# A 4-bit code table built from two-slope planes with min and max: four ScalarE and four VectorE operations per chunk in place of six and six, and no GpSimd subtraction

## The reference

```python
w = NF4[codes]                      # 16 values from -1.0 to 1.0
w = w.reshape(O, I // 64, 64) * scales[:, :, None]
q, k, v = (lin_lora(x, W, A, B) for each of three)      # 512 x 512 each
o  = lin_lora((q + k + v) / 3, W_o, ...);   x1 = x + o
g, u = lin_lora(x1, W_g), lin_lora(x1, W_u)             # 1792 x 512 each
d  = lin_lora(silu(g) * u, W_d, ...);       r = x1 + d  # W_d is 512 x 1792
x  = layernorm(x + r)
x  = layernorm(x + ffn(x))          # ffn: one more coded matrix, absmax scales
```

## Time and profile before

| | us |
|---|---|
| median of 3 runs | 570.43 (570.41 to 571.09) |
| span of the profiled execution | 569.6 |
| TensorE matmul busy | 506.0 (89%) |
| VectorE busy | 434.0 (76%) |
| ScalarE busy | 362.1 (64%) |
| GpSimd busy | 335.2 (59%) |

### The profile page before, as it was taken

The page is one execution under the profiler, slowest core; times in us unless marked ns, Lnnn a source line. Parts: engine busy times, 40 slices in busy tenths (PEclk is TensorE's granted clock), DMA queues, the critical chain, the costliest instruction groups (busy, mean ns, idle before and its releaser), DMA issues.

```text
span 569.6 us, 8051 instructions
## 1 busy us (share of the span) xinstructions
PE 506.0 (89%) x2260; PEld 398.3 (70%) x2260; DVE 434.0 (76%) x821; ACT 362.1 (64%) x655; POOL 335.2 (59%) x318
## 2 busy tenths in 40 slices
PE   0465549988999999999999999989999799999995
PEld 0142338766788878777777787768888588888874
DVE  7899988999857779989899899257745885465542
ACT  8899956698757668878789686216768542232121
POOL 5889824179857678979879789314739811020011
PEclk9986659999999999999999999999999999999999
DMA  8732402033323122323323230064000000010011
GB/s 249 256 100 86 129 18 67 13 99 119 100 69 93 56 93 96 107 82 112 106 91 108 80 112 20 1 249 148 2 0 2 0 2 1 18 39 20 0 37 38
DMA packets 20379, 42.97 MB, mean 75 GB/s; under 512 B 3312, under 2 KB 3440, under 8 KB 19824
## 3 DMA queue, kind: packets, MB, share of 16 engines
q1 hardware_dynamic: 20112, 42.09, 23.1%
q0 software_dynamic: 224, 0.38, 0.3%
HBM read 40.36 MB, written 2.10 MB: 75 GB/s over the span
## 4 chain that ended last, share of the span: by engine, by line
PE 68%; POOL 15%; issue 13%; ACT 2%; DVE 2%; POOLq 0%; ACTq 0%; DVEq 0%
PE bank L870 58%; POOL wf L615 6%; PE bank L1002 3%; POOL wf L623 3%; POOL wf L628 2%; PE bank L961 2%; POOL wf L634 2%; PE bank L987 1%; PE bank L1106 1%; PE bank L888 1%; PE bank L895 1%; ACT prob L831 1%; ACT pT_hi L681 0%; PE bank L889 0%; DVE rmax L1312 0%
## 5 line engine op out<-in xcount | busy, mean ns | idle before, releaser
L702 ACT ACTIVATE bank<-code 128x512 f32<-128x512 int32 x372 | 207.8, 595 | 25.1 <-DVE half L1165 12.1
L615 POOL TENSOR_TENSOR wf<-halves 128x512 f32<-128x512 f32 x62 | 80.1, 1292 | 78.5 <-DVE halves L1169 77.3
L870 PE MATMUL bank<-x_hi,gu_hi 128*128 128x512 f32 x224 | 89.5, 399 | 2.7 <-POOL gu_lo L641 2.7
L664 POOL TENSOR_TENSOR rstd<-veps,neg_half 128x1 f32<-128x1 f32 x32 | 17.6, 549 | 121.7 <-issue 110.5
L870 PE MATMUL bank<-x_lo,gu_hi 128*128 128x512 f32 x224 | 87.3, 390 | 0.0
L870 PE MATMUL bank<-x_hi,gu_lo 128*128 128x512 f32 x224 | 87.3, 390 | 0.0
L1165 DVE SCALAR_TENSOR_TENSOR half<-half,bank 128x512 f32<-128x512 f32 x124 | 81.5, 680 | 3.6 <-ACT bank L702 3.6
L1163 DVE SCALAR_TENSOR_TENSOR half<-code,bank 128x512 f32<-128x512 int32 x124 | 79.2, 680 | 6.5 <-ACT bank L702 5.1
L1169 DVE TENSOR_TENSOR halves<-half,bank 128x512 f32<-128x512 f32 x124 | 79.3, 680 | 0.0
L623 POOL TENSOR_TENSOR wf<-wf,scale 128x512 f32<-128x512 f32 x50 | 65.3, 1305 | 3.9
L870 PEld LDWEIGHTS bank<-x_hi,gu_hi 128*128 128x128 f32 x224 | 42.1, 188 | 16.6 <-issue 6.3
(11 more groups left out here) (195 smaller groups left out, 1133.7 us busy)
## 6 DMA issues: line engine op xcount, KB each, us to landing
code<-codes SPq DMA_DIRECT2D x62, 256.0 KB, 2.7
scale<-scales SPq DMA_DIRECT2D x100, 128.0 KB, 2.9
xs<-xT SPq DMA_DIRECT2D x1, 2048.0 KB, 12.9
ea_raw<-ex_A SPq DMA_DIRECT2D x1, 2048.0 KB, 9.6
eb_raw<-ex_B SPq DMA_DIRECT2D x1, 2048.0 KB, 7.7
out<-rows SPq DMA_DIRECT2D x8, 256.0 KB, 2.0
bgu_raw<-loB_gu SPq DMA_DIRECT2D x1, 1792.0 KB, 10.5
wqkv_raw<-w_qkv SPq DMA_DIRECT2D x1, 768.0 KB, 4.0
```

What stands on the lines that cost most here:

```text
L615: pool.tensor_tensor(w, halves[:, j % 2, 0, :], halves[:, j % 2, 1, :], ALU.subtract).then_inc(diff_done, 1)
L664: pool.tensor_tensor(rstd[:, s:s + 1], veps[:, s:s + 1], neg_half[:, :], ALU.pow)\
L702: nc.scalar.activation(plane[m % RING_PLANE][:, :], src, func, bias=float(start), scale=float(slope)).then_inc(plane_ready, 1)
L870: last = nc.tensor.matmul(ps, a, b, start=start and i == 0 and n == 0, stop=stop and i == len(terms) - 1 and n == 2)
```

## The change

The 16 table values are now built from three bent lines ("two-slope planes": ScalarE's Prelu with a slope on either side, `BEND_LOW`, `BEND_LAST`, `BEND_TOP`), one Relu and the code itself, joined by two min and two max. All values are scaled by `GAIN`, so that the code itself is one of the lines; the factor is taken out again in `m1`, `p`, `silu`, `h`, `down` and the layer norm of the ffn, and a unit matrix times `GAIN` (`gain_eye`) takes the place of `ident` there. The chunk's last VectorE operation is an item of its own, `out`, that stands one half later; merges and splits stand one half later too. GpSimd only multiplies.

```diff
 def half(c, part):
     if part == 1:
+        due.append([1, ("out", c)])
         if c in MERGED:
-            due.append([2, ("merge", c)])
+            due.append([3, ("merge", c)])
         if c in SPLIT:
-            due.append([3 if c in MERGED else 2, ("split", c)])
+            due.append([4 if c in MERGED else 3, ("split", c)])
...
-plane = bank[0:RING_PLANE]
+last_ps, mid_ps, top_ps = bank[0:3]
...
 # ScalarE
+act.wait_ge(eye_in, 16)
+nc.scalar.activation(gain_eye[:, :], ident[:, :], ACT.Copy, scale=GAIN).then_inc(gain_set, 1)
...
+if item[2] == 0:
+    act.wait_ge(codes_in[j % RING_CODES], 16 * (j // RING_CODES + 1))
+    if j >= 2:
+        act.wait_ge(low_done, j - 1)
+    bent_plane(bent[:, j % 2, :], src, BEND_LOW, bent_ready)
+    if j:
+        act.wait_ge(low_done, j)
+    bent_plane(last_ps[:, :], src, BEND_LAST, last_ready)
+    if j:
+        act.wait_ge(clip_done, j)
+    nc.scalar.activation(mid_ps[:, :], src, ACT.Relu, bias=..., scale=...).then_inc(mid_ready, 1)
+else:
+    if j:
+        act.wait_ge(value_done, j)
+    bent_plane(top_ps[:, :], src, BEND_TOP, top_ready)
...
 # VectorE
+    if item[2] == 0:
+        dve.wait_ge(bent_ready, j + 1)
+        dve.wait_ge(last_ready, j + 1)
+        nc.vector.scalar_tensor_tensor(lj, bent[:, j % 2, :], ..., last_ps[:, :], ALU.add, ALU.min).then_inc(low_done, 1)
+        dve.wait_ge(mid_ready, j + 1)
+        nc.vector.scalar_tensor_tensor(mid_ps[:, :], code[...], float(CODE_SHIFT), mid_ps[:, :], ALU.add, ALU.max).then_inc(mid_done, 1)
+    else:
+        nc.vector.scalar_tensor_tensor(lj, lj, float(BEND_LAST[3]), mid_ps[:, :], ALU.add, ALU.min).then_inc(clip_done, 1)
+elif kind == "out":
+    dve.wait_ge(top_ready, j + 1)
+    dve.wait_ge(clip_done, j + 1)
+    nc.vector.scalar_tensor_tensor(value[:, j % 2, :], top_ps[:, :], float(BEND_TOP[3]), low[:, j % 2, :], ALU.add, ALU.max).then_inc(value_done, 1)
...
 # GpSimd
-pool.tensor_tensor(w, halves[:, j % 2, 0, :], halves[:, j % 2, 1, :], ALU.subtract).then_inc(diff_done, 1)
-pool.tensor_tensor(w, w, scale[:, i % RING_CODES, :], ALU.mult).then_inc(done, 1)
+pool.tensor_tensor(w, v, scale[:, i % RING_CODES, :], ALU.mult).then_inc(scaled_done, 1)
...
 # VectorE: merge (v, o, d) and h; down is changed in the same way
-nc.vector.tensor_tensor(w, lora_ps[:, :], w, ALU.add)
+nc.vector.scalar_tensor_tensor(w, lora_ps[:, :], GAIN, w, ALU.mult, ALU.add)
-nc.vector.tensor_tensor(a, a, unit_ps[(2 * n + 1) % 3][:, :], ALU.mult)
+nc.vector.scalar_tensor_tensor(a, unit_ps[(2 * n + 1) % 3][:, :], 1.0 / GAIN, a, ALU.mult, ALU.mult)
```

More of the change, by code:

```diff
@@ L58, with line, crossing, bend @@
        0.7229568362236023, 1.0]
-def line(sign, a, b):
-    slope = sign * (NF4[b] - NF4[a]) / (b - a)
-    return slope, sign * NF4[a] - slope * a
-UPPER = [line(1, 8, 9), line(1, 10, 11), line(1, 12, 13), line(1, 14, 15)]
-LOWER = [line(-1, 6, 5), line(-1, 4, 3), line(-1, 2, 1), (1.5 * (NF4[0] - NF4[1]), -NF4[0])]
+def line(a, b):
+    slope = (NF4[b] - NF4[a]) / (b - a)
+    return slope, NF4[a] - slope * a
+def crossing(left, right):
+    at = (right[1] - left[1]) / (left[0] - right[0])
+    return at, left[0] * at + left[1]
+def bend(left, right):
+    at, value = crossing(left, right)
+    return GAIN * right[0], -GAIN * right[0] * at, left[0] / right[0], GAIN * value
+FREE = 0.5
+GAIN = 1.0 / line(10, 11)[0]
+FIRST = ((line(1, 2)[0] * FREE + line(1, 2)[1] + 1.0) / FREE, -1.0)
+BEND_LOW = bend(line(3, 4), line(5, 6))
+BEND_LAST = bend(FIRST, line(1, 2))
+BEND_TOP = bend(line(12, 13), line(14, 15))
+RELU_MID = (GAIN * line(8, 9)[0], GAIN * line(8, 9)[1])
+CODE_SHIFT = GAIN * line(10, 11)[1]
+def lut_table(prelu_as_relu=False):
+    table = []
+    for c in range(16):
+        def plane(b):
+            x = b[0] * c + b[1]
+            return max(x, 0.0) + (0.0 if prelu_as_relu else min(x, 0.0) * b[2])
+        low = min(plane(BEND_LOW) + BEND_LOW[3] - BEND_LAST[3], plane(BEND_LAST))
+        mid = max(c + CODE_SHIFT, max(RELU_MID[0] * c + RELU_MID[1], 0.0))
+        clip = min(low + BEND_LAST[3], mid)
+        table.append(max(plane(BEND_TOP) + BEND_TOP[3], clip) / GAIN)
+    return table
 GROUPS = [range(f, f + 2) for f in range(0, NF, 2)]
@@ L98 @@
 RING_W = 3
-RING_PLANE = 3
 RING_H = 5
@@ L272, in build @@
         scale = at("scale", 6, [P, RING_CODES, 512])
-        half = at("half", 12, [P, 2, 512])
-        halves = at("halves", 16, [P, 2, 2, 512])
+        low = at("low", 12, [P, 2, 512])
+        bent = at("bent", 16, [P, 2, 512])
+        value = at("value", 20, [P, 2, 512])
         wf = at("wf", 24, [P, RING_W, 512])
@@ L601, in _ @@
             pool.memset(neg_half[:, :], -0.5).then_inc(neg_half_set, 1)
-            mults = 0
+            sums = 0
             for item in filter(None, V):
                 kind = item[0]
-                if kind == "lut" and item[2] == 1:
+                if kind == "out":
                     c = item[1]
                     j = CHUNKS.index(c)
-                    w = wf[:, j % RING_W, :]
-                    pool.wait_ge(lut_step, 6 * (j + 1))
+                    w, v = wf[:, j % RING_W, :], value[:, j % 2, :]
+                    pool.wait_ge(value_done, j + 1)
                     if j >= RING_W:
@@ L1152, in _ @@
                     j = CHUNKS.index(c)
-                    src = code[:, j % RING_CODES, :]
-                    dve.wait_ge(codes_in[j % RING_CODES], 16 * (j // RING_CODES + 1))
-                    for i in range(3 * item[2], 3 * item[2] + 3):
-                        m, side = 6 * j + i, i % 2
-                        lines = (UPPER, LOWER)[side]
-                        ps, acc = plane[m % RING_PLANE][:, :], half[:, side, :]
-                        dve.wait_ge(plane_ready, m + 1)
-                        if m >= 2:
-                            dve.wait_ge(lut_step, m - 1)
-                        if i < 2:
-                            ins = nc.vector.scalar_tensor_tensor(acc, src, float(lines[3][0]), ps, ALU.mult, ALU.max)
-                        elif i < 4:
-                            ins = nc.vector.scalar_tensor_tensor(acc, acc, float(lines[3][1]), ps, ALU.add, ALU.max)
-                        else:
-                            if j >= 2:
-                                dve.wait_ge(diff_done, j - 1)
-                            ins = nc.vector.tensor_tensor(halves[:, j % 2, side, :], acc, ps, ALU.max)
-                        ins.then_inc(lut_step, 1)
+                    lj = low[:, j % 2, :]
@@ L1191, in _ @@
                     dve.wait_ge(xhi_done, item[1] + 1)
-                    low(x_lo[:, k, tk], xs[:, k, tk], x_hi[:, k, tk], xlo_done)
+                    rest(x_lo[:, k, tk], xs[:, k, tk], x_hi[:, k, tk], xlo_done)
                 elif kind == "m1":
@@ L1225, in _ @@
                     dve.wait_ge(p_ready, NB)
-                    low(lb_dl[:, :], lb_d[:, :], lb_dh[:, :], dprep_done)
+                    rest(lb_dl[:, :], lb_d[:, :], lb_dh[:, :], dprep_done)
                 elif kind == "p":
@@ L1256, in _ @@
                     dve.wait_ge(down_added, (gi - 1) * TT + t + 1)
-                    nc.vector.tensor_tensor(rows[:, t, :], down_bank(gi, t)[:, :], rows[:, t, :], ALU.add)\
+                    nc.vector.scalar_tensor_tensor(rows[:, t, :], down_bank(gi, t)[:, :], 1.0 / GAIN, rows[:, t, :],
+                                                   ALU.mult, ALU.add)\
                         .then_inc(down_added, 1)
```

153 lines of the change are left out of this document (93 added, 60 removed).

## The result

| | before | after |
|---|---|---|
| median, same chip | 570.76 (570.41 to 571.95, 4 runs) | 591.62 (589.37 to 595.71, 4 runs) |
| ratio, 95% interval | | 1.0366 (1.0325 to 1.0407) |
| span of the profiled execution | 569.6 | 590.0 |

What follows compares the result with a forecast made beforehand. VectorE was taken to limit the first part and TensorE the stretch from about 150 to 370 us. The terms 4.5 + 0.7 + 11.1 = 16.3 gave 587 us by the runs, range 577 to 594.

Steps and rivals of the forecast that it cites:

- Term 1: Start: ScalarE's first plane waits for the unit matrix, at about 9.4 us instead of 3.42; +4.5 together with Term 2.
- Term 2: First part's chunk loop: fourth plane waits for `out`, 3.69 per chunk, 17.0 per group against 16.26; +4.5 with Term 1.
- the rival of dearer planes: Prelu planes or handoffs cost more; 0.1 on three planes gives +4.8; 592 to 598, chance 0.12.
- the rival on the other side: Chunk goes at the pace of the work, 2.40 instead of 3.69: −4.3, 566; chance of faster 0.06.
- threshold of 2.67 a chunk: Time per chunk below which the changed kernel was said to be faster than before.
- Term 3: Between first part and hidden blocks: later merges delay d2's lora product and u2's low part; +0.7, between 0 and 2.6.
- Term 4: Hidden blocks: TensorE's lora products wait for merges behind h, 0.55, 1.44 or 2.36 each; +11.1.
- The table's own pace costs nothing in the hidden blocks: Hidden blocks: a four-chunk block needs about 17 us of table work, TensorE over 19, so no cost.

Runs made afterwards that it cites:

- The start alone: Kernel before plus one wait of ScalarE for the unit matrix ahead of its first plane: 575.29 us, ratio 1.0066.
- `out` at once: Changed kernel with `out` directly behind the chunk's second half, and merges and splits at the distances of before: 556.53 us, ratio 0.9730.
- the earlier start: Changed kernel with the scaled unit matrix made ahead of v0's operations instead of ahead of all: 591.63 us, ratio 1.0344.
- the later lora product: Changed kernel with TensorE's lora product of the next d behind the next `gate` instead of ahead of it: 577.77 us, ratio 1.0106.
- the run with the fourth plane beside it: Changed kernel with ScalarE's fourth plane issued at the place of that chunk's `out`, behind the next chunk's first three planes: 582.50 us, ratio 1.0170.

## Why the prediction was right, and where its terms were off

The forecast (slower, 12 to 21 by first part and lora waits) is what happened: +20.4 by spans, where the sum said +16.3.

**Term 1, right.** First plane at 9.66, said 9.4. The start alone costs 3.8 to 4.4, shown on the kernel before.

**Term 2, right.** The loop is 3.64, said 3.69, and it is the loop described: breaking it in ScalarE's queue alone gives 2.56, breaking it with `out` at once 2.77. L1225 of chunk 15 ends at 73.24, said 73.6; four x_lo take 3.61, said 3.4. Terms 1 and 2 together are 5.16, said 4.5: the table ends 0.4 sooner than said, and the way from there to the last product is 1.0 longer (9.97, said 9.0). A Prelu plane takes 0.59 into PSUM and 0.62 into SBUF on average, the Relu plane 0.59, so the rival of dearer planes falls. By 3.64 the rival on the other side falls too. Its threshold of 2.67 a chunk did not hold, though. With late merges the kernel was slower than before at 2.77 (579), as it says, but also at 2.56 (582), where it says faster: the first unit gained 11.3 and not 16 · 1.08 = 17.3, since the merges stretch the chunks around them (mostly 3.1 to 3.9), and the clock behind the waits is not in it. And at 2.77 with early merges the kernel was faster (557), since there the waits went too.

**Term 3, mis-sized.** Said +0.7, measured 2.6, the upper end of its bounds. The mechanism was there (d2's lora product waits 2.65, said 2.7), and it did absorb the waits of before for g2 and u2; u2's low part is waited for 1.26 (4.3 less 2.95 was said). What was missing is mainly 1.6 us of low clock behind d2's wait.

**Term 4, right in sum by luck, wrong in its parts.** Said +11.1, measured 11.9 (from +8.0 to +19.9). Each of the waits is shorter than said, 0.39 for 0.55 and 1.28 for 1.44; from the end of `up` to the lora product it is 2.65, said 2.73, and the lateness grows by 0.47 and 1.36. The waits of f were said to be 2.36 and are 1.65 (3.01 from the end of `up`, said 3.65): most of that is L1254, which took 0.33 and not the 0.88 of the earlier trace rows. Here is VectorE around it in block 7:

```profile
261.98 0.69 DVE L1220 SCALAR_TENSOR_TENSOR bank<-code,bank 128x512 f32<-128x512 int32 x1
262.58 0.68 DVE L1249 SCALAR_TENSOR_TENSOR wf<-bank,wf 128x512 f32<-128x512 f32 x1
263.30 0.33 DVE L1254 TENSOR_TENSOR wf<-wf,gain_eye 128x128 f32<-128x128 f32 x1
```

And GpSimd beside it:

```profile
262.21 1.27 POOL L689 TENSOR_TENSOR h_lo<-act_f,h_hi 128x512 fp32r<-128x512 f32 x1 [4.09 <-ACT h_hi L723]
```

GpSimd ends at 263.48, and L1254 ends at 263.63, 0.15 later. In the kernel before GpSimd's subtraction beside the same operation ran from 248.71 to 250.00, and the operation ended at 250.14: again 0.14 behind GpSimd. With `out` at once L1254 starts at 233.35 with no GpSimd operation beside it, and takes 0.29. So the 0.88 is not a price of the operation: it tells how long GpSimd's read still lasted when it started. The Trainium skill (SBUF — State Buffer, Who interferes with whom) has it so: a VectorE instruction with two SBUF inputs contends with a GpSimd instruction that reads SBUF, and the port pair that they share is an exclusive lock. These times agree. I had used that rule for x_lo and not for this row.

What the waits of f were short of, the low clock made up: 3.1 us behind those of blocks 9 and 11. This step was nowhere in the prediction: I counted TensorE's waits and not what it does after them.

**The last block, missed.** +0.5: a `down` of block 13 starts at 381.75, when VectorE's addition (L1319, from 381.01) is done, and that stands behind the merge of the fourth f chunk, whose L1254 ends at 381.09.

**Hidden costs.** "The table's own pace costs nothing in the hidden blocks" holds: without merge waits the lateness no longer grows through ten blocks.

So the total came out within 0.8% partly by luck, with two errors of about 2 us (f's merges) and 5 us (clock) of opposite signs.

## What to carry to other kernels

Fewer operations help only if the queue lets them run: an engine's fourth operation that waits for a buffer which exists once holds the next chunk's first ones behind it, and here a third or more of the loop was idle on both engines; look for the one operation that waits for what it isn't needed for, and move it, or consume its buffer at once. A consumer moved later "by one half" must be checked against each in-order queue that waits for it: behind h it sat on TensorE's path. And when the bounding engine has no idle time, price a new wait on TensorE above its length, since the clock may fall behind it.

## What the hardware showed that I had not expected

- **The clock behind short waits.** TensorE was busy at 2.4 GHz, waited 1.65 us, and ran 1.2 GHz for the next three or four us (matmuls 0.43 apart for 0.227), at a loss of 1.6, as long as the wait itself. It is not a fixed price: in the changed kernel it came behind two of three waits of 1.65 and behind neither of 1.28, with the earlier start behind all three of 1.65 and one of 1.29; in the kernel before with late merges behind one of two waits of 1.88. Removing the waits removed it in each run (clock 1.00 from 150 to 370 us in the kernel before and in every one with early merges or the later lora product; 0.97 or 0.98 in all five with late merges and the lora product ahead of `gate`). Ahead of 150 us, which these means leave out, it also fell at the wait for d0's lora inputs in four runs (1.97 to 2.99 us), while the same wait of 1.97 in the changed kernel was not followed by it. What decides which wait is followed by it stays open; an earlier start by 3.9 us changed which ones were.
- **An operation that reads what the one ahead wrote.** On VectorE such an operation starts 0.78 to 0.79 after it (38.95 to 39.74 above), and 0.60 after one that it doesn't depend on. With `out` between the halves (33.11 to 35.08 in the run with the fourth plane beside it) only 0.60 to 0.75 is seen; four operations take 2.77 in the one order and 2.56 in the other. With L1254 behind L1249, which writes what it reads, it is 0.72 (262.58 to 263.30).
- **Small steps of 0.43** stand ahead of the first `down` of five units in the two kernels with `out` late and merges early. The trace shows what is waited for: the `down` starts when VectorE has added the one before it to `rows` (in the one kernel L1319 runs from 209.83 to 210.51, and the `down` starts at 210.56), and its first matmul comes 0.52 after the one ahead of it, not 0.227. Why VectorE is that late there was not tested.
